# Grouped attention in fp32 from three-part products: the probabilities turned as fp16 halves by the DMA engines

## What is computed

```python
q = (hidden_states @ Wq).reshape(B, S, N_HEADS, HEAD_DIM)          # 4, 256, 16, 128
k = (encoder_hidden_states @ Wk).reshape(B, S_enc, N_KV_HEADS, HEAD_DIM)   # 4, 1601, 4, 128
v = (encoder_hidden_states @ Wv).reshape(B, S_enc, N_KV_HEADS, HEAD_DIM)
q = rms_norm(q, q_norm_w)
k = rms_norm(k, k_norm_w)
k = jnp.repeat(k, groups, axis=2)
v = jnp.repeat(v, groups, axis=2)
scores = jnp.einsum('bqhd,bkhd->bhqk', q, k) * scale
probs = jax.nn.softmax(scores, axis=-1)
out = jnp.einsum('bhqk,bkhd->bqhd', probs, v)
return out.reshape(B, S, N_HEADS * HEAD_DIM) @ Wo
```

## Time and profile before

| | |
|---|---|
| median of 3 runs | 1645.3 us (1642.59 to 1646.03) |
| the profiled execution | 1644.82 us, its span 1642.7 us |
| TensorE busy | 1443.0 us, 88% of the span |
| VectorE, ScalarE, GpSimd busy | 1161.6 us (71%), 982.1 us (60%), 570.5 us (35%) |
| mean granted clock of TensorE | 0.955 |
| first and last exp of grouped attention begin | 460.3 us, 1547.1 us |

### The profile page before, as it was taken

How to read it: one execution, slowest core, us unless ns; L and a number is a source line. 1 busy time by engine, 2 the same in 40 slices (tenths; PEclk the granted TensorE clock), 3 DMA queues, 4 the chain that set the end, 5 groups by cost and what they waited for, 6 DMA issues and landing times. The chain is left out here.

```text
span 1642.7 us, 27599 instructions
## 1 busy us (share of the span) xinstructions
PE 1443.0 (88%) x10080; PEld 1347.7 (82%) x10080; DVE 1161.6 (71%) x2372; ACT 982.1 (60%) x2065; POOL 570.5 (35%) x477
## 2 busy tenths in 40 slices
PE   6998378887679899999999899999989999999945
PEld 5888268776569898899999899999989999999823
DVE  4765688887567776667777667776766777677657
ACT  4564177887356565665656566566656656656536
POOL 3342154443355232342323343332234323322135
PEclk9999589999799999999999999999999999999968
DMA  6241479998223020101102011010101101001010
GB/s 202 77 168 58 153 246 295 299 299 282 61 46 78 20 70 10 50 20 27 43 8 70 20 40 42 8 43 16 59 20 39 43 8 43 21 7 27 23 52 26
DMA packets 83691, 128.05 MB, mean 78 GB/s; under 512 B 17284, under 2 KB 63496, under 8 KB 83176
## 3 DMA queue, kind: packets, MB, share of 16 engines
q1 hardware_dynamic: 79000, 113.84, 21.8%
q0 software_dynamic: 4560, 12.46, 3.1%
HBM read 114.28 MB, written 11.99 MB: 77 GB/s over the span
## 5 line engine op out<-in xcount | busy, mean ns | idle before, releaser
L1836 ACT ACTIVATE ga_pT<-ga_ps_t 128x512 fp32r<-128x512 f32 (+1 forms) x512 | 243.9, 516 | 256.5 <-PE ga_ps_t L2070 255.7
L1971 DVE TENSOR_TENSOR ga_pT<-ga_ps_t,ga_pT 128x512 fp32r<-128x512 f32 (+1 forms) x512 | 280.3, 583 | 94.3 <-ACT ga_pT L1836 92.3
L1844 ACT ACTIVATE ga_probs<-ga_ps_s,ga_neg_max 128x1200 f32<-128x1200 f32 (+1 forms) x256 | 235.7, 927 | 90.0 <-DVE ga_neg_max L1992 89.7
L2070 PE MATMUL ga_ps_t<-all_eye,ga_probs 128*128 128x128 f32 (+1 forms) x1664 | 227.0, 274 | 9.7 <-DVE ga_pT L1971 9.6
L2070 PEld LDWEIGHTS ga_ps_t<-all_eye,ga_probs 128*128 128x128 f32 (+1 forms) x1664 | 192.8, 141 | 19.7 <-DVE ga_pT L1971 12.6
L1987 DVE TENSOR_REDUCE ga_part_max<-ga_ps_s 128x1 f32<-128x1200 f32 x128 | 178.8, 1397 | 12.0 <-PE ga_ps_s L2021 10.5
L1738 POOL TENSOR_TENSOR ga_oT<-ga_out_n,ga_oT 128x256 fp32r<-128x256 f32 x64 | 47.6, 744 | 394.9 <-ACT ga_oT L1859 394.9
L2021 PE MATMUL ga_ps_t<-side_w_kv,side_encT 128*128 128x256 f32 (+1 forms) x1170 | 164.4, 290 | 13.9 <-DVE ga_pT L1971 8.6
L2021 PE MATMUL ga_ps_m<-ga_pT,ga_v 128*128 128x256 f32 (+1 forms) x1248 | 174.0, 286 | 2.6 <-DVE ga_pT L1971 2.4
L2021 PE MATMUL ga_ps_m<-ga_pT,side_v 128*128 128x256 f32 (+1 forms) x1248 | 174.6, 287 | 0.6 <-DVE ga_pT L1971 0.5
L2021 PEld LDWEIGHTS ga_ps_t<-side_w_kv,side_encT 128*128 128x128 f32 (+1 forms) x1170 | 147.0, 188 | 23.5 <-DVE ga_pT L1971 11.4
(11 more groups left out here) (274 smaller groups left out, 2617.4 us busy)
## 6 DMA issues: line engine op xcount, KB each, us to landing
ex_raw<-in_L_ffn_packed SPq DMA_DIRECT2D x63, 704.0 KB
side_w_q_raw<-in_L_xattn_Wq SPq DMA_DIRECT2D x16, 512.0 KB
side_w_q_raw<-in_L_xattn_Wo SPq DMA_DIRECT2D x16, 512.0 KB, 4.6
ga_inv_rows<-ga_inv_row SPq DMA_DIRECT2D x64, 128.0 KB, 3.1
mix_y_rows<-ex_y SPq DMA_DIRECT2D x63, 128.0 KB
side_enc<-in_ctx_turned SPq DMA_DIRECT2D x12, 512.0 KB, 5.3
ca_keys<-in_ctx_turned SPq DMA_DIRECT2D x12, 464.0 KB, 6.1
ca_cache<-in_ctx SPq DMA_DIRECT2D x4, 1024.0 KB, 8.3
```

The source lines that it names most:

```text
L1836: nc.scalar.activation(dst(HI), src, ACT.Copy, scale=scale).then_inc(read, 1)
L1844: nc.scalar.activation(dst, src, ACT.Exp, bias=neg_max[:, n % 2:n % 2 + 1], accum_out=half_sum[:, n % 4, k:k + 1]).then_inc(exped, 1)
L1971: nc.vector.tensor_tensor(dst(LO), src, f32(dst(HI)), ALU.subtract).then_inc(empty, 1)
L2070: mm = nc.tensor.transpose(out[0:top, i * P:(i + 1) * P], probs[step % PB][:, tile * P:tile * P + top], eye[:, :])
```

## The change

In grouped attention the transposes on TensorE are dropped.

- `probs_high` (ScalarE): behind both exps of step n it waits for that step's inverse sum (times 2^15) and writes probabilities times it as fp16 into `halves[n % 2]`, HI part, in 1,024 and 577 columns. `probs_low` (VectorE) computes the product again, subtracts the HI part and writes the LO part, fp16, in the same two pieces.
- `turn_probs` (SP): for each step two DMAs with transpose, HI and LO, 128 x 1,664 fp16 each, into `pT`, now fp16 with a copy for odd and for even units. `weigh` waits for both steps of the unit (`turned_through`).
- `invert` runs every step and for one column each; VectorE's loop is now `largest(n)`, the entries of `plan[n - 1]`, `invert(n)`, `probs_low(n)`; in the first step of a group the entries come ahead of `largest`. ScalarE's loop is `exp`, `probs_high`, `take_values` or `split_result`, then the ring jobs.
- The values are scaled by `v_scale` to fit fp16, and the result by `out_scale`. The scale comes from a bound: largest sum of squares of a context row (`enc_squares`, twelve squares with sums in cached attention) by the largest sum of squares of a column of Wv (products in `experts`), through a chain over all engines. VectorE's first `weights_low` and ScalarE's later work stand behind it (`KEY_SCALE` is now the last of `dve_routed`).
- `normalize_out` and `invert_rows` go. `probs` has two buffers, `oT` six head slots.
- The small jobs are spread anew: `kv` two to a step, `kT` in steps 6 and 7, `y` in steps 6 and 7, `split_out` in step 2. `pieces` are 4, 3, 3, 3 tiles. The first small job stands between the two pieces of values.

The diff, cut to its core:

```diff
+                nc.scalar.activation(v[:, HI, at, :], cache[:, at, :], ACT.Square,
+                                     accum_out=routing.enc_squares[:, 3 * b + h:3 * b + h + 1]).then_inc(squared, 1)
+                act.wait_ge(squared, 3 * b + h + 1)
...
+            pool.wait_ge(dve_routed, BOUND)
+            nc.gpsimd.tensor_tensor(root[:, :], bound[:, :], half_power[:, 0:1], ALU.pow).then_inc(pool_ready, 1)
...
     def step_plan(n):
...
+        jobs = prepared(n) if n < N + DRAIN - 1 else [("y", t, GROUPS - 1) for t in range(QT)]
+        assert sum(e[0] in RING for e in jobs) <= TB
+        values = weighed(n)
+        return ([("scores", 0, n)] if n < N else []) + values[0:1] + jobs[:1] + values[1:2] + jobs[1:]
...
-        pT = sb("pT", [P, 2, KT, S], F32R)
+        pT = [sb(f"pT{i}", [P, 2, KT, S], F16) for i in range(2)]
+        halves = [sb(f"halves{i}", [P, 2, PADDED], F16) for i in range(2)]
...
+            def turn_probs(n, part, ready):
+                u, t = n // QT, n % QT
+                sp.wait_ge(ready, 2 * n + 2)
+                if u >= 2:
+                    sp.wait_ge(out_ready, u - 1)
+                sp.dma_start(pT[u % 2][:, part, :, t * P:(t + 1) * P], halves[n % 2][:, part, :], transpose=True
+                             ).then_inc(turned[n % TURNS], 16)
...
+            def probs_high(n):
+                act.wait_ge(inverted, n + 1)
+                if n >= 2:
+                    act.wait_ge(*turned_through(n - 2))
+                for a, z in ((0, SPLIT), (SPLIT, KV)):
+                    nc.scalar.activation(halves[n % 2][:, HI, a:z], probs[n % PB][:, a:z], ACT.Copy,
+                                         scale=inv_sum[:, n % 2:n % 2 + 1]).then_inc(high, 1)
...
+            def probs_low(n):
+                if n >= 2:
+                    dve.wait_ge(*turned_through(n - 2))
+                for k, (a, z) in enumerate(((0, SPLIT), (SPLIT, KV))):
+                    dve.wait_ge(high, 2 * n + k + 1)
+                    nc.vector.scalar_tensor_tensor(halves[n % 2][:, LO, a:z], probs[n % PB][:, a:z],
+                                                   inv_sum[:, n % 2:n % 2 + 1], halves[n % 2][:, HI, a:z],
+                                                   ALU.mult, ALU.subtract).then_inc(low, 1)
...
+            for n in range(N + DRAIN + 1):
+                first_of_group = n % STEPS == 0
+                if n < N and not first_of_group:
+                    largest(n)
+                if n:
+                    for e in plan[n - 1]:
+                        entry(e)
+                if n < N and first_of_group:
+                    largest(n)
                 if n < N:
-                    largest(n)
-                for e in plan[n]:
-                    entry(e)
+                    invert(n)
+                    probs_low(n)
...
-                elif kind == "pT":
...
             def weigh(half, piece, u):
                 if piece == 0:
-                    pe.wait_ge(*emptied(("pT", (QT - 1, 2 * half + 1), u)))
-                    if half == 0 and u:
-                        pe.wait_ge(u_here, u)
+                    if half == 0:
+                        for t in range(QT):
+                            pe.wait_ge(*turned_through(QT * u + t))
+                        if u:
+                            pe.wait_ge(u_here, u)
```

More of the change, by code:

```diff
@@ L933, in experts @@
         passed = sb("passed", [SLOTS, E])
+        value_w = sb("value_w", [P, DC, wv.shape[1]])
+        ones = sb("ones", [P, P])
+        w_largest = sb("w_largest", [P, 1])
+        row_largest = sb("row_largest", [P, 1])
+        largest = sb("largest", [1, 1])
+        bound = sb("bound", [P, 1])
+        root = sb("root", [P, 1])
         block_expert = sb("block_expert", [SLOTS, 1])
@@ L1307, in _ @@
             mm.then_inc(pe_routed, 1)
-            pe.wait_ge(dve_routed, TOKENS)
+            pe.wait_ge(act_routed, VALUE_W_SQUARED)
+            pe.wait_ge(pool_ready, 8)
+            for c in range(DC):
+                mm = nc.tensor.matmul(ps_w, ones[:, :], value_w[:, c, :], start=c == 0, stop=c == DC - 1)
+            mm.then_inc(pe_routed, 1)
+            pe.wait_ge(dve_routed, ROW_LARGEST)
+            nc.tensor.transpose(ps_largest, row_largest[:, :], eye[:, :]).then_inc(pe_routed, 1)
+            pe.wait_ge(dve_routed, LARGEST)
+            nc.tensor.matmul(ps_spread, ones[0:1, :], largest[:, :], start=True, stop=True).then_inc(pe_routed, 1)
+            pe.wait_ge(dve_routed, BOUND)
             def beside_products(e):
@@ L1454, in prepared @@
+        if 0 < g < GROUPS and s in (6, 7):
+            jobs = [("y", s - 6, g - 1)] + jobs
         row, at = divmod(g + 2, G)
         if at == 0 and row < B:
-            late = late + {6: [("norm", 0, row)], 7: [("xT", 0, row)]}.get(s, [])
+            if s == 0:
+                jobs = jobs + [("norm", 0, row)]
+            if s == 2:
+                jobs = [("xT", 0, row)] + jobs
         row, at = divmod(g + 1, G)
         if at == 0 and row < B and s < 4:
-            late = late + [("enc", (0, 1, 3, 2)[s], row)]
+            jobs = jobs + [("enc", (0, 1, 3, 2)[s], row)]
@@ L1460, in prepared @@
         if n in COMBINE:
-            late = late + [("combine", COMBINE[n], 0)]
-        return early, late
+            jobs = jobs + [("combine", COMBINE[n], 0)]
+        return jobs
     def step_plan(n):
-        turns, values = turned_probs(n), weighed(n)
-        early, late = prepared(n) if n < N + DRAIN - 1 else ([], [])
-        if n == N + DRAIN - 1:
-            late = [("y", t, GROUPS - 1) for t in range(QT)]
-        return (([("scores", 0, n)] if n < N else []) + turns[0:2] + early + values[0:1] + late[:1] + values[1:2]
-                + turns[2:4] + late[1:])
+        jobs = prepared(n) if n < N + DRAIN - 1 else [("y", t, GROUPS - 1) for t in range(QT)]
@@ L1566, in grouped_attention @@
         inverted = sem("inverted")
-        inv_out = sem("inv_out")
-        inv_in = sem("inv_in")
+        high = sem("high")
+        low = sem("low")
+        turned = [sem(f"turned{i}") for i in range(TURNS)]
         out_ready = sem("out_ready")
         u_here = sem("u_here")
-        out_here = sem("out_here")
         out_hi = sem("out_hi")
@@ L1685, in _ @@
             nc.gpsimd.memset(f32(kT[1][:, :, KV:COLS_EVEN]), 0.0).then_inc(cleared, 1)
+            for part in (HI, LO):
+                for i in range(2):
+                    nc.gpsimd.memset(halves[i][:, part, KV:PADDED], 0.0).then_inc(cleared, 1)
             def split_q(g):
@@ L1887, in _ @@
                     split_result((n - 5) // 2)
+                for e in plan[n]:
+                    if e[0] == "enc":
+                        split_encoder(e[1], e[2])
+                    elif e[0] in RING and e[0] != "y":
+                        ring(e)
                 if n == 0:
@@ L2105, in weigh @@
                     top = P if tile < FULL else REST
-                    mm = product(ps_m[:, :], lambda s: values[0:top, s, tile, :], lambda s: pT[0:top, s, tile, :],
+                    mm = product(ps_m[:, :], lambda s: values[0:top, s, tile, :], lambda s: pT[u % 2][0:top, s, tile, :],
                                  tile == 0, tile == KT - 1)
```

259 lines of the change are left out of this document (129 added, 130 removed).

## The result

After the change the kernel takes 1730.12 us (median of 4 runs, 1729.41 to 1732.58), before it 1643.94 us in the same comparison: a ratio of 1.0531, 95% interval 1.0505 to 1.0558. It is 86 us slower; the forecast was 1688, 43 slower, with 1570 to 1790 as the range and 1650 to 1725 as the forecast's own. The profiled execution spans 1727.5 us (before 1642.7).

A forecast was written before the change was run, and what follows sets the result against it. TensorE bound the kernel; after the change a VectorE-ScalarE chain would. Groups 20, first sixteen steps 4, row changes 8, cached attention 8 and experts 3 make 43 us on 1644.8: 1688, range 1570 to 1790 (its own 1650 to 1725).

The forecast's parts named there:

- The bound: Grouped attention: the bound moves from TensorE, 8.70 us a step, to a serial chain over VectorE and ScalarE, 7.53.
- The collisions with GpSimd: Grouped attention: GpSimd's result lows, norms and weight split delay VectorE's low halves, 9.1 us a group.
- the jobs ahead of the first largest: First step of a group: VectorE's entries come before largest and add about 1.7 us.
- Rival 1: Grouped attention: GpSimd is seldom in the way, a group takes 62.2 us; total put at 1600 us; chance 0.33.
- Light groups: Grouped attention: first sixteen steps +4 us, for combine's operations; group 15 +1.4 like other groups.
- Row changes: Grouped attention: three changes of row, with statistics and three big GpSimd splits, +8 us beside 1.4 a group.
- Quiet groups: Grouped attention: a group takes 71.0 us, 1.4 more than before; 14 groups are +20 us.
- Cached attention: Twelve squares on ScalarE ahead of TensorE's work: between 0 and 16 us, taken as 8.
- Experts: Expert stage: a chain for the scale of the values before the first weight split, 1 to 8 us, taken as 3.
- The end: End of attention: the DMA turn adds some 4 us where evictions and the product by 1/sum go: 0.
- Rival 2: Grouped attention: DMA engines or SP's issue bound the step, over 4.4 us a half; total 1826 to 2466; chance 0.16.
- Rival 3: Grouped attention: the low half lands late, or TensorE loses its clock; half a microsecond a step, total 1750; chance 0.08.

The follow-up runs named there:

- the runs with the chain cut: After with VectorE writing the low half of step n-1 behind largest(n): ahead of the small jobs 1779.72 us, behind them 1677.22 us.
- the third experiment: After, but from the fifth step on the DMA of a low half turns one tile of 128 keys instead of thirteen: 1730.26 us.
- the kernel of 1608 us: After with low half n-1 behind largest(n) and the jobs, GpSimd's encoder split first, TensorE's first job ahead of the values in odd steps: 1608.2 us.

## Why the prediction came out half as large as the result

**The bound** was named rightly: TensorE at 79% in place of 96%, both halves hidden, the step a chain over VectorE and ScalarE. Its links are 2.11, 1.96, 0.45, 1.25 and 1.93 us against 2.09, 1.93, 0.40, 1.17 and 1.94: 7.70 in place of 7.53, 0.17 a step. Most of it is the hops between engines: the first high half itself takes 1.15 us, against my 1.14.

**The collisions with GpSimd** were the cost that decides, as the cut of its work shows. The lows of the result cost 0.48 and not 0.75 (8.18 against 7.70); the steps with norms take 8.96, 9.62 and 9.65 against my 9.13, 9.83 and 9.73. What I had too much there (9.1 for 6.6), the chain (1.4 a group) and the jobs ahead of the first largest (2.0 in place of 1.7) had too little: that a quiet group takes 70.6 to 71.0 us, forecast 71.0, is in part luck. Rival 1 fell: GpSimd is in the way 6.6 us a quiet group. I had it decide at some 8 us of collisions a group; by my own terms it is 6 (69.6 less 61.9 and a fourteenth of the 23 elsewhere), and by the runs some 1, for without nearly all of them the kernel takes 1628, 13 less than before in the same comparison.

**Where the 41 us were missed** (1729.41 for the profiled execution against 1688, which puts it above my own range of 1650 to 1725) is in what I subtracted from, and in what I did not list:
- *Light groups* (0 with 1, and 15), +20.4 in place of 4 + 1.4. Group 15 has no next group to prepare, group 0 only queries; before, where TensorE's work was the bound, most of their steps took 5.9 to 6.9 us. The chain has the same length with or without small jobs, so they cannot go under 7.6 to 7.7. I applied +1.4 to group 15 and priced the first sixteen steps only for combine. This is 15 us, and the trace of before held it. No run isolates it; it is read from the step lengths, and from the runs with the chain cut, whose group 15 takes 5.5 us a step where nothing waits for the DMA; with the low turn short as well, it takes 39.7 us in place of 55.3.
- *Row changes*, groups 2, 3, 6, 7, 10 and 11: +38.5 in place of 16.4. Before, the change cost 7 us in groups 2, 6 and 10; that is milder now. The stall in groups 3, 7 and 11 is new, 11 us a time, and comes from an entry that the change moved by one step past an entry of GpSimd. I had costed the moved norm as time of GpSimd, and not as a wait with the encoder's split queued behind it. Turned round, it gives 34 us back. This is the largest step that failed.
- *Quiet groups*, +2.0 in place of +1.4 each, some 4 us over seven. The mean of the earlier trace rows over 92 steps, 69.6, contains the row changes of before; a quiet group took 68.3.

**Other stages.** Cached attention +7.8 (8), of which the squares are 6.7 or a little more. Experts -1.8 (3): VectorE's first split of weights begins at 213.97 in place of 198.53, and yet ScalarE's last copy of weights comes only 5.8 us later than before (415.1 against 409.3), less than the 7.8 by which the stage starts late. Before, ScalarE waited 14.4 us in all for loads of weights, now 2.7; that is where the buffer that I counted as lost was made up. The end +5.9 (0). I left the landing uncovered there, as no scores hide it:

```profile
1634.95 6.62 PE L2094 MATMUL ga_ps_m<-ga_pT,ga_v 128*128 128x256 f16 x39 [6.77 <-DMA ga_pT<-ga_halves]
1646.27 4.61 PE L2094 MATMUL ga_ps_t<-ga_w_out,ga_oT 128*128 128x256 f32 x24 [4.70 <-POOL ga_oT L1790]
```

From the last largest to the start of the last output products it is 21.7 us in place of 18.3. The other 2.5 us are in the last stage, whose code is the same. In its last 18.5 us the granted clock is 0.68, before 0.80, and its last 16 products take 3.32 us in place of 2.11; why the clock is lower there stays open.

**Rival 2** asked for over 4.4 us a half. The DMA engines need 2.1 us; near my low end, 1.4, and far from the 7.5 of the earlier trace rows. The low end had weak ground: the loads of the earlier trace rows come from DRAM, not from SBUF as a half does, so they are not "between the same ends". The Trainium skill ("DMA: Bandwidth & Descriptors", Latency and other measured facts) gives 261 GB/s for a turning DMA with a non-contiguous middle dimension, measured on one kernel; the trace has 204 here, a fifth less. The cycle count of the Trainium skill's page is, by its own words, time in the sequencer without the moving of data, so my 3 to 5.5 us are to be held against the issue on SP, and that took 1.49 us in the median. The time to land, 3.9 us, is in neither figure, and it is what bound the odd steps once the chain was cut. Rival 3's first half was thus right one kernel later: hidden in after, as the third experiment shows, it was 95 us of waits in 800 when the low half was written a step later. Its second half came true in the rows, the clock being 0.92 against 0.99, but it did not lengthen the quiet steps of after (8.19 us at 0.79, 8.18 at 1.00); like the first half, it costs one kernel later.

## What to carry to other kernels

When work goes off the engine that sets the end, write out the serial chain of one step over the others, and compare it with the lightest stretch of the kernel as well as with its mean: a chain doesn't get shorter where there is less to do. For every entry that moves on an engine that runs its list in order, ask what is queued behind its wait, and not only how long it takes. A transfer that is hidden has a distance, from where its source is written to where it is read; each reordering that frees the writer spends some of it, and buffers shared by three engines spend it too.

## What the hardware showed that I had not expected

- A turn by DMA of 128 x 1,664 fp16 within SBUF goes in 1,664 packets of 256 bytes at 204 GB/s: 2.1 us of all 16 engines, 1.49 us of issue on SP, 3.9 us from issue to landing. With 38% fewer packets in queue 1 the operations of VectorE on the same halves took the same time to a few ns in the median (1285).
- The collision of VectorE and GpSimd slows both: beside a low half, GpSimd's product of keys by their norms took 2.84 us in place of 1.90, the low half of the result 0.93 in place of 0.74, and a pair of low halves 3.66 in place of 2.02 (2.50 beside a low half of the result; at the most 5.20, in step 2 of groups 3, 7 and 11, beside two big operations of GpSimd):

```profile
1017.81 3.66 DVE L2067 SCALAR_TENSOR_TENSOR ga_halves<-ga_probs,ga_inv_sum,ga_halves 128x1024 f16<-128x1024 f32 x2 [1.28 <-ACT ga_halves L1907]
```

- A wait of TensorE can cost twice. Behind waits of 2.2 to 2.9 us its clock fell to 1.2 GHz in some groups and not in others. In the kernel of 1608 us such a step takes 10.4 us in place of 8.8; in after, where another chain is the bound, it takes the same 8.2.
